# Interleaved node rows: partition p of each 512-node block holds nodes 4p to 4p+3, and the turns read every fourth column

## The reference

```python
# L0
u = par_u[0] * par_u[1] * (diag_u[:, None] * x[:2048] @ W_u) + x[:2048]
i = par_i[0] * par_i[1] * (diag_i[:, None] * x[2048:] @ W_i) + x[2048:]
e = concatenate([u, i])
h = A @ (A.T @ e)
x = norm(x + norm(h) * gamma + beta + x)
# L1
x = norm(x + 1 - 0.1 * x - 0.01 * sum(x * (A @ x), axis=1))
# L2
z = concatenate([x, (A @ x + x) / deg]) @ W + b
x = norm(x + relu(z) / |relu(z)|)
# L3: T0 = x, T1 = A @ x, T2 = 2 A T1 - T0, T3 = 2 A T2 - T1
x = norm(x + sum_k(Tk @ weight[k]) + bias)
```

## Time and profile before

| | |
|---|---|
| three runs | 1519.85, 1520.79 and 1522.48 us, median 1520.79 |
| the profiled execution | 1520.75 us |
| its span, first to last instruction and transfer | 1518.9 us |
| PE busy | 1492.4 us, 98% |
| PEld busy | 696.8 us, 46% |
| DVE, ACT, POOL busy | 611.9, 251.5, 61.3 us |
| moved by DMA | 519.11 MB in 122,435 packets |

### The profile page before, as it was taken

The page is one execution under the profiler, slowest core; times in us unless marked ns, Lnnn a source line. Parts: engine busy times, 40 slices in busy tenths (PEclk is TensorE's granted clock), DMA queues, the critical chain, the costliest instruction groups (busy, mean ns, idle before and its releaser), DMA issues.

```text
span 1518.9 us, 17591 instructions
## 1 busy us (share of the span) xinstructions
PE 1492.4 (98%) x6638; PEld 696.8 (46%) x6638; DVE 611.9 (40%) x1335; ACT 251.5 (17%) x492; POOL 61.3 (4%) x66
## 2 busy tenths in 40 slices
PE   8999999999999999999999999999999999999998
PEld 6555554555554533324444344443444444444332
DVE  5755565655555577423331544233111021110342
ACT  3343333334343410000100001000000000000000
POOL 0000000000000012100000111000000000000010
PEclk8999999999999999999999999999999999999999
DMA  9899999999999989999788598786388869988997
GB/s 305 319 395 410 411 410 412 412 409 413 412 409 411 357 339 382 421 422 405 294 316 291 192 329 301 290 298 247 140 327 313 301 226 349 337 313 297 366 421 267
DMA packets 122435, 519.11 MB, mean 342 GB/s; under 512 B 21068, under 2 KB 21108, under 8 KB 72308
## 3 DMA queue, kind: packets, MB, share of 16 engines
q1 hardware_dynamic: 105264, 412.64, 72.5%
q10 hardware_dynamic: 17092, 105.38, 16.6%
HBM read 411.82 MB, written 106.17 MB: 341 GB/s over the span
## 4 chain that ended last, share of the span: by engine, by line
issue 99%; POOLq 0%; POOL 0%; DVE 0%
POOL power_out L421 0%; POOLq L419 0%; POOLq L421 0%; DVE rows L907 0%; POOL ident L414 0%; POOLq L416 0%; POOL ident L416 0%; POOLq L1150 0%
## 5 line engine op out<-in xcount | busy, mean ns | idle before, releaser
L729 PE MATMUL ps_u<-blk,vectors 128*128 128x512 f32 (+1 forms) x2000 | 721.9, 594 | 1.1 <-DMA blk<-a_transposed 1.1
L729 PEld LDWEIGHTS ps_u<-blk,vectors 128*128 128x128 f32 (+1 forms) x2000 | 288.6, 171 | 387.2 <-issue 382.1
L475 ACT ACTIVATE blk<-ps_turn 128x512 f32<-128x512 f32 x400 | 206.1, 605 | 327.0 <-PE ps_turn L553 324.2
L582 PE MATMUL ps_h<-blk,u_rows 128*64 128x512 f32 x720 | 164.4, 599 | 0.0
L1072 DVE TENSOR_TENSOR part<-part,ps_u 64x512 f32<-64x512 f32 (+1 forms) x45 | 30.9, 686 | 315.8 <-PE ps_u L729 314.7
L819 DVE TENSOR_REDUCE row_part<-blk 128x4 f32<-128x2048 f32 x68 | 152.4, 2279 | 0.4
L553 PE MATMUL ps_turn<-ident,blk 128*128 128x128 f32 x1088 | 130.0, 279 | 3.9 <-DMA blk<-in_adj 3.9
L553 PEld LDWEIGHTS ps_turn<-ident,blk 128*128 128x128 f32 x1088 | 121.7, 144 | 24.1 <-issue 19.5
L803 DVE TENSOR_TENSOR part<-part,ps_h 128x512 f32<-128x512 f32 x80 | 55.0, 688 | 185.5 <-PE ps_h L582 185.5
L565 PE MATMUL ps_u<-blk,e 128*64 128x512 f32 x544 | 123.6, 594 | 0.8 <-DMA blk<-in_adj 0.8
L421 POOL TENSOR_TENSOR power_out<-power_in,minus_half 128x4 f32<-128x4 f32 x60 | 60.6, 1010 | 1454.0 <-DVEq L870 1454.0
(11 more groups left out here) (110 smaller groups left out, 566.3 us busy)
## 6 DMA issues: line engine op xcount, KB each, us to landing
blk<-a_transposed SPq DMA_DIRECT2D x291, 1024.0 KB, 6.4
a_transposed<-blk ACTq DMA_DIRECT2D x100, 1024.0 KB, 9.6
blk<-in_adj SPq DMA_DIRECT2D x68, 1024.0 KB, 22.4
nat_far<-in_adj SPq DMA_DIRECT2D x32, 1024.0 KB, 22.2
rows<-in_x SPq DMA_DIRECT2D x10, 128.0 KB, 9.0
out<-rows SPq DMA_DIRECT2D x10, 128.0 KB, 3.6
w3x<-in_L_gnn_weight ACTq DMA_DIRECT2D x6, 16.0 KB, 9.5
w2x<-in_L_gnn_W ACTq DMA_DIRECT2D x4, 16.0 KB, 9.6
```

The source lines that it names most:

```text
L475: nc.scalar.activation(blk[:, n % RING, t, :], ps_t[t][:, :], ACT.Copy)\
L582: mm = pe.matmul(ps_h[n % 2][half(t), :], u_rows[:, t, :], blk[:, n % RING, t, :], start=t < 2, stop=t >= TB - 2)
L729: mm = pe.matmul(acc, left, tiles[:, t, :], start=first, stop=last)
```

## The change

All tensors over nodes take another order inside a block: partition p holds the nodes 4p to 4p + 3. The four rows of x, and of the output, that a partition holds are then neighbours in DRAM, so that a packet has 1 KB and not 256 B. A row piece of A stays at 2 KB. The diagonals are loaded as 10 rows of 512 and not as 40 of 128. Rows lie so by the loads alone; for columns, the transposes have to take nodes t, 4 + t, 8 + t and so on together, so each of the 16 per block, and each of the four in `u_turn_back`, reads its stationary operand with a step of four elements (16 bytes). `turn_diag` becomes four matmuls of 10 rows, and the two DVE operations behind it write `diag` with a step.

```diff
-    a_blocks = adj.rearrange("(t p) j -> p t j", p=P)
-    x_rows = x.rearrange("(t p) f -> p t f", p=P)
-    out_rows = out.rearrange("(t p) f -> p t f", p=P)
+    a_blocks = adj.rearrange("(i p t) j -> p i t j", p=P, t=TB)
+    x_rows = x.rearrange("(i p t) f -> p i t f", p=P, t=TB)
+    out_rows = out.rearrange("(i p t) f -> p i t f", p=P, t=TB)
...
-        diag_flat = sb("diag_flat", [NT, P])
+        diag_flat = sb("diag_flat", [NB, BLK])
...
-                    sp.dma_start(rows[:, tiles, :], x_rows[:, tiles, :]).then_inc(x_loaded[i], 16)
+                    sp.dma_start(rows[:, tiles, :], x_rows[:, i]).then_inc(x_loaded[i], 16)
...
-                sp.dma_start(nat(n), a_blocks[:, i * TB:(i + 1) * TB, j * BLK:(j + 1) * BLK])\
+                sp.dma_start(nat(n), a_blocks[:, i, :, j * BLK:(j + 1) * BLK])\
...
-                sp.dma_start(out_rows[:, i * TB:(i + 1) * TB, :], rows[:, i * TB:(i + 1) * TB, :])\
+                sp.dma_start(out_rows[:, i], rows[:, i * TB:(i + 1) * TB, :])\
...
-            const(diag_flat[0:UT, :], diag_u.rearrange("(t p) -> t p", p=P))
-            const(diag_flat[UT:NT, :], diag_i.rearrange("(t p) -> t p", p=P))
+            const(diag_flat[0:UB, :], diag_u.rearrange("(i n) -> i n", n=BLK))
+            const(diag_flat[UB:NB, :], diag_i.rearrange("(i n) -> i n", n=BLK))
...
+            def every_fourth(columns, t):
+                return columns.rearrange("p (q t) -> p t q", t=TB)[:, t]
...
             def turn_diag():
-                pe.matmul(diag_in, diag_flat[:, :], ident[0:NT, 0:NT], start=True, stop=True)\
-                    .then_inc(diag_turned, 1)
+                for t in range(TB):
+                    mm = pe.matmul(diag_in[:, t * NB:(t + 1) * NB], every_fourth(diag_flat[:, :], t), ident[0:NB, 0:NB],
+                                   start=True, stop=True)
+                mm.then_inc(diag_turned, 1)
...
-                        mm = pe.transpose(ps_t[t][:, c * P:(c + 1) * P], nat(n)[:, c, t * P:(t + 1) * P],
+                        mm = pe.transpose(ps_t[t][:, c * P:(c + 1) * P], every_fourth(nat(n)[:, c, :], t),
                                           ident[:, :])
...
-                    mm = pe.transpose(ps_u[j % 2][:, t * P:(t + 1) * P], u_turned[:, t * P:(t + 1) * P], ident[:, :])
+                    mm = pe.transpose(ps_u[j % 2][:, t * P:(t + 1) * P], every_fourth(u_turned[:, :], t), ident[:, :])
...
-            V.tensor_scalar(diag[:, 0:UT], diag_in[:, 0:UT], par_prod[:, 0:1], None, ALU.mult)
-            V.tensor_scalar(diag[:, UT:NT], diag_in[:, UT:NT], par_prod[:, 1:2], None, ALU.mult)
+            diag_tiles = diag[:, :].rearrange("p (i t) -> p t i", t=TB)
+            diag_blocks = diag_in.rearrange("p (t i) -> p t i", t=TB)
+            V.tensor_scalar(diag_tiles[:, :, 0:UB], diag_blocks[:, :, 0:UB], par_prod[:, 0:1], None, ALU.mult)
+            V.tensor_scalar(diag_tiles[:, :, UB:NB], diag_blocks[:, :, UB:NB], par_prod[:, 1:2], None, ALU.mult)
```

More of the change, by code:

```diff
@@ L44, in build @@
     UB = diag_u.shape[0] // BLK
-    UT = UB * TB
     SWEEPS = 6
```

## The result

The changed kernel takes 1542.31 us (median of 4 runs, 1541.56 to 1542.54), the kernel before 1521.63 us beside it. The ratio is 1.0132, with a 95% interval of 1.0119 to 1.0145: 1.3% slower, 20.7 us. The forecast was 1527.3 us: the right side, less than a third of the size, and outside the range.

What follows compares the result with a forecast made beforehand. PE was taken as the bound. To the span of 1518.9 us came 6.4 for stepped transposes, 0.4 for the start, less 0.2 for the output: 1525.5, and with 1.85 beyond the span 1527.3 us (+0.43%), range 1524 to 1530.

Steps and rivals of the forecast that it cites:

- What bounds the kernel: Pass over A, 100 to 540 us: PE is the bound; loads of A have some 8 us of lead to spare.
- The transposing load before: A's transposes: a load needs about 60 ns, hidden behind the MATMUL's 109.3 ns with about 50 ns to spare.
- Rows 7 are the model: Stepped transposes run like line 646's plain float32 matmul, 111.7 ns each: 3.9 us, with first loads 6.4 us; chance 0.44.
- The diagonals: Start of the kernel: one matmul becomes four, six more load-and-matmul pairs of 0.2 us at clock 0.50, 1.2 us on PE.
- the halving: Start: 0.8 us more work ahead of the clock's rise at 18.3 us moves behind it, takes half as long: +0.4 us.
- x in long packets: Start: x's first load with 128 packets, not 512, lets A's first block come 0 to 1 us earlier; 0.4 taken.
- A's loads: Loads of A's blocks keep 2 KB pieces and their count; costed at nothing, with 8 us of lead as cover.
- free step: Transposing loads: reads don't depend on where a word lies, all else stays, 1520.9 us; chance 0.30.
- The outgrown load: Transposes: the load outgrows the matmul, +105 us (1626 us) at 173 ns or +179 us (1700 us) at quarter pace; chance 0.13.
- slower loads of A: Pass over A: addresses spread otherwise over DRAM slow the loads by a tenth, +14 us, 1535 to 1541 us; chance 0.05.
- The clock: Start: the clock stays up or rises sooner, winning 1.9 to 4.5 us; 1516.4 to 1519.0 us with a free step; chance 0.08.
- The rules weighed: Transposing loads: the skill's 107 ns for 128 columns would leave no shadow, half pace 213 ns, some 170 us in sum.

Runs made afterwards that it cites:

- PE alone: Computation left out, only stretches of transposes or plain matmuls on data at rest, against no kernel; 109 ns a transpose at step 1, 120 ns at step 4.

## Why the prediction was wrong

- **What bounds the kernel**: right. PE was the bound and stayed it, the lead held, and no wait for A's blocks appeared beyond that for the first.
- **The transposing load before** (60 ns alone, 50 ns of shadow): right. With 64 rows step 1 ran at 63 ns a transpose.
- **"Rows 7 are the model"**: this step failed. That the step would take the load from double pace to about single pace, and past its shadow, was the right mechanism. But I took the pace of a plain load for that of a stepped one. Line 646's loads are contiguous, and such loads follow PE's clock (112 ns at full clock, 213 at half); a load with a step of four takes 120 ns for its 128 columns at either clock. That the fetch of single words sets this pace is a guess that no run shows, and the 113 and 114 ns at steps 8 and 3 speak against one price for each word. The term was 1,640 by 2.4 ns; it measured 1,640 by 120 - 109.3 = 10.7 ns, 17.5 us. The first load of a run was late by 0.05 us as forecast, 2.5 us. Together 20 us, and the step alone gave 1541.50 - 1521.29 = 20.2; that the two agree so closely is in part luck, as the interval of the ratio runs from 17.8 to 22.5 us, and in that kernel's trace the pass over A was 18.5 us longer than before.
- I had written that the load costs every further nanosecond 1,640 times once past 109, and then laid the forecast just at that edge. A price right at an edge, with 1.6 us for each nanosecond, deserved a range up to the next bound, 173 ns; 1531 us was only the case in which the model held exactly.
- **The diagonals**: near in size, for another reason. I priced six more passes at 0.2 us, 1.2 us, and halved it. But the two of before had run beside those of `times_w`, which start at 12.84 us against 12.83, and the eight of the diagonals alone did not; the net was 1.4 us, and 0.84 us were left when `u_part` began. The ratio of 1.0017 allows 1.1 to 4.1 us, so the halving can't be claimed. In the changed kernel the eight passes stand where the granted clock is 1.00 (the second of the windows further down) and still take 14.98 - 13.02 = 1.96 us:

```profile
13.02 2.03 PE L528 MATMUL ps_u<-ident,diag_flat 10*128 10x10 f32 x8
14.98 0.32 PE L549 MATMUL ps_u<-w,u_turned 64*128 64x64 f32 x1
```

Their loads are plain and have the step of four, and eight of the 233 ns that PE alone showed for such a load make 1.86 us. That such work "takes half as long" at full clock doesn't hold for them.
- **x in long packets**: the last store landed after 1.7 us, 1.8 were forecast. The 0.4 us at the start did not come: the changed kernel's first block was turned from 9.61 us, and before from 9.22. So "*A's loads*: costed at nothing" missed 0.4 us at the first block; for the rest of the pass it held.
- **The rivals**: no free step. The outgrown load was the true kind, and its price lay between the forecast and that rival's lower one. (Its upper price has a slip: a quarter of the pace of a 60 ns load is 240 ns, not 218.) The time of 1542.3 us is nearest to the 1535 to 1541 us of slower loads of A, but that rival is out: without the step the same loads land after 22.2 us and the ratio is 1.0016. The clock did rise earlier for some of the start in the changed kernel, and fell again (windows of it, below); `u_part` still began at 21.05 us and not at 20.16.

```profile
9.60:13.20 3.60, 3.59 (x17) 3.46 (x17) 0.00 (x0) 1.87 (x4) 0.00 (x0) 0.57 1.07 370
13.20:15.20 2.00, 2.00 (x12) 1.98 (x13) 0.12 (x1) 0.52 (x1) 0.00 (x0) 1.00 1.06 381
15.20:18.60 3.40, 3.40 (x24) 3.33 (x23) 2.63 (x7) 1.37 (x3) 0.00 (x0) 0.64 1.06 383
```

- **The rules weighed**: the P / 1.2 ns of the Trainium skill (TensorE: Matmul & The Clock Gate, LDWEIGHTS) doesn't hold for the transposing load, 60 to 63 ns for 128 columns here. The two hits in 16 bytes of Advanced Engine Details and Errata of the Trainium skill, Memory Cachelines, agree with the moved operand (113 ns with step 2, 226 with step 4) and with plain loads (118 and about 233), and not with the transposing load, where step 2 costs all that step 4 does.

In the whole times the parts don't add up to the digit: the step alone 1.0132, the rest alone 1.0016, both 1.0132, with intervals that cover the difference. At the end of the pass over A the traces add up: 18.5 us later with the step alone, 2.0 with the rest alone, 20.35 with both. What follows that point, which the change touches only in its stores, takes 977.8 us before, 978.2 in the changed kernel and without the step, and 980.6 with the step alone; that spread hides a part of 2 us. Nor is the start alike in every profile: with the step alone `u_part` began at 19.15 us, 1.0 us earlier than in the kernel before. No version here beats the kernel before, and the changed kernel with its diagonals transposed can't be told from the changed one by its time. Not tried: putting single transposes of the real kernel between long matmuls. There the long matmuls run in pairs on halves of the array (two start every 0.43 us, where PE alone started one), which such an order would break up.

## What to carry to other kernels

A transpose on PE is a load that hides behind a short MATMUL. Before its columns are given a step, ask what pace the load has alone and how long the MATMUL beside it is: behind 128 moved columns a step of four costs 10% of each transpose, behind 512 nothing. A nicer layout for a few DMAs (loads of 128 KB that nobody waits for) has to be weighed by the count of what it changes elsewhere, here ten x loads against 1,640 loads on the bound engine. And where a term sits at an edge, give it its range from what lies beyond the edge.

## What was not expected of the hardware

- A stepped load doesn't slow down with PE's clock: 120 ns for 128 columns at 1.00 and at 0.51, and 233 ns at either clock in a plain matmul. At a clock of 0.50 a transpose has the longer cover, and the step was free: the first block's 16 transposes take 3.69 us with a step of two and 3.68 us without.
- The price isn't monotonic in the step: per transpose 109 ns at step 1, 120 at 2, 114 at 3, 120 at 4, 116 at 5, 113 at 8, and in the real kernel a step of eight lost 4.9 us where two lost 18.6 and four 20.2. PE alone at full clock also ran steps that the text above leaves out: about 134 ns at 6, 122 at 7, 126 at 12, 112 at 16 and 111 at 32, and a step of four costs the same from columns 1, 2 and 3 as from column 0. Why is open.
- Four matmuls of 10 rows in a row took 1.81 us and cost PE 1.4 us more than one of 40 rows, whose two passes ran beside their neighbours.
- In the three kernels that load A in the new order the first block was turned from 9.58 to 9.62 us; in the six others with A's old order, and in the kernel before, from 9.04 to 9.22. A's order goes with the delay; x's packets alone and the diagonals alone do not bring it. These are single profiles, and its mechanism was not sought.
